# One pass over x removed, the hidden rows of the graph part made in the first attention stage, the preparation reordered

## The reference, cut to what matters

```python
xn = layernorm(x, eps=1e-5)
# graph part: rows that are gathered along the edges
h = relu(xn @ W1 + b1) @ W2 + b2            # 512 -> 256 -> 512
gnn = h + segment_sum(h[dst], src)
# attention part, one batch of 6250 tokens
k, q, v = split(layernorm(xn, eps=1e-3) @ kqv_w + kqv_b)
kp = exp(k @ w.T - |k|^2 / 2) / 16          # 256 features; qp in the same way from q
D = qp . sum_t kp ;  kptv = v.T @ kp
y = v + ((qp @ kptv.T) / D) @ proj_w + proj_b
mix = y + gelu(layernorm(y) @ mlp_w1) @ mlp_w2
x = x + gnn + mix
# then a Haar transform with two layers on its low half, on layernorm(x), added to x
```

## Time and profile before

| | us |
|---|---|
| median of 3 runs (2145.37 to 2147.61) | 2145.99 |
| the profiled execution | 2143.18 |
| its span, first to last instruction | 2141.4 |
| TensorE busy | 1913.4 (89%) |
| VectorE busy | 1184.4 (55%) |
| ScalarE busy | 493.2 (23%) |
| GpSimd busy | 1006.1 (47%) |
| mean granted TensorE clock | 0.954 |

### The profile page before, as it was taken

How to read it: one execution, slowest core, us unless ns; L and a number is a source line. 1 busy time by engine, 2 the same in 40 slices (tenths; PEclk the granted TensorE clock), 3 DMA queues, 4 the chain that set the end, 5 groups by cost and what they waited for, 6 DMA issues and landing times.

```text
span 2141.4 us, 24742 instructions
## 1 busy us (share of the span) xinstructions
PE 1913.4 (89%) x8639; PEld 1455.0 (68%) x8639; DVE 1184.4 (55%) x2337; ACT 493.2 (23%) x1083; POOL 1006.1 (47%) x1054
## 2 busy tenths in 40 slices
PE   3866699999979999999999997599999999999775
PEld 2755688888767777777777775466666666776432
DVE  3456398987234555555555554134444456665776
ACT  2445433333210111111111110111111122232222
POOL 3232200000056777777777777477777754410000
PEclk8878799999999999999999999699999999999997
DMA  7434522223223444444444445455555544432222
GB/s 207 165 120 160 160 85 68 80 81 93 69 79 110 134 137 137 137 136 137 137 136 136 137 128 171 134 156 160 162 165 161 179 150 156 155 125 99 91 96 82
DMA packets 90895, 278.93 MB, mean 130 GB/s; under 512 B 19183, under 2 KB 20719, under 8 KB 90774
## 3 DMA queue, kind: packets, MB, share of 16 engines
q1 hardware_dynamic: 46358, 153.81, 21.5%
q0 software_dynamic: 44416, 123.56, 21.4%
HBM read 232.47 MB, written 44.83 MB: 129 GB/s over the span
## 4 chain that ended last, share of the span: by engine, by line
PE 74%; DVE 10%; DMA 9%; issue 4%; ACT 1%; POOL 1%; DVEq 0%; SPq 0%; ACTq 0%
PE bank L777 8%; PE bank L784 8%; PE bank L683 8%; PE turn_bank L683 7%; PE bank L558 5%; PE bank L560 5%; PE bank L559 5%; PE bank L717 4%; PE bank L647 3%; DMA sb_step<-x_t 3%; DVE sb_weights L1084 3%; DMA out<-sb_step 2%; PE bank L696 2%; PE bank L698 2%; PE bank L697 2%
## 5 line engine op out<-in xcount | busy, mean ns | idle before, releaser
L496 POOL DMA_INDIRECT sb_weights<-hidden_rows,sb_weights x880 | 910.5, 1035 | 428.5 <-issue 245.2
L558 PE MATMUL bank<-sb_w_parts,sb_x_high 128*125 128x256 f32 (+1 forms) x700 | 242.2, 346 | 5.1 <-DVE sb_x_low L1151 5.1
L683 PE MATMUL bank<-sb_weights 128*125 128x257 f32 x880 | 231.7, 385 | 16.5 <-DVE sb_acc L1361 12.5
L1361 DVE TENSOR_TENSOR sb_acc<-sb_acc,bank 125x257 f32 x220 | 92.6, 421 | 264.9 <-PE bank L683 256.2
L560 PE MATMUL bank<-sb_w_parts,sb_x_low 128*125 128x256 f32 (+1 forms) x700 | 231.3, 330 | 0.0
L559 PE MATMUL bank<-sb_w_parts,sb_x_high 128*125 128x256 f32 (+1 forms) x700 | 231.3, 330 | 0.0
L683 PE MATMUL turn_bank<-sb_weights 128*125 128x257 f32 x880 | 229.8, 382 | 1.6 <-DMA sb_weights<-hidden_rows,sb_weights 1.4
L683 PEld LDWEIGHTS bank<-sb_weights 128*125 128x125 f32 x880 | 154.7, 187 | 69.3 <-issue 51.3
L777 PE MATMUL bank<-sb_weights 128*128 128x250 f32 x800 | 180.0, 378 | 15.7 <-issue 15.0
L683 PEld LDWEIGHTS turn_bank<-sb_weights 128*125 128x125 f32 x880 | 160.2, 187 | 33.1 <-issue 5.9
L784 PE MATMUL bank<-sb_weights,sb_step 128*125 128x512 f32 x400 | 177.8, 593 | 0.8 <-ACT sb_weights L1029 0.7
(11 more groups left out here) (229 smaller groups left out, 3056.1 us busy)
## 6 DMA issues: line engine op xcount, KB each, us to landing
sb_step<-x_t SPq DMA_DIRECT2D x75, 500.0 KB, 7.2
sb_step<-x SPq DMA_DIRECT2D x75, 500.0 KB
sb_weights<-hidden_rows,sb_weights POOLq DMA_INDIRECT x880, 3.7
y_rows<-sb_step SPq DMA_DIRECT2D x25, 500.0 KB
sb_step<-y_rows SPq DMA_DIRECT2D x25, 500.0 KB
z_rows<-sb_step SPq DMA_DIRECT2D x25, 500.0 KB
sb_step<-z_rows SPq DMA_DIRECT2D x25, 500.0 KB
out<-sb_step SPq DMA_DIRECT2D x25, 500.0 KB
```

The costliest lines, as they stand in the source:

```text
L496: pool.indirect_dma_start(out=slot(n, h), out_offset=None, in_=table, in_offset=bass.IndirectOffsetOnAxis(ap=row_of[:, n, h:h + 1], axis=0 ...
L558: pe.matmul(bk, high, rhs(0, c), start=c == 0, stop=False)
L683: mm = pe.matmul((BE, BH)[n % 2][0:P, 0:RW], hit[n // BP % 2][:, n % BP * 2 + h, :], slot(n, h), start=h == 0, stop=h == 1)
L1361: dve.tensor_tensor(dst, dst, (BE, BH)[n % 2][0:P, 0:RW], ALU.add).then_inc(g_add, 1)
```

## The change: what it does

- Pass 0 is gone. Steps of passes 1 and 2 alone load x.
- The W1 weights (r) lie between the k weights and the kqw weights in `w1_parts`, so that r and kqw come from one product of 512 columns (256 + 256) into a whole bank. It also waits until VectorE has read the r rows of the step before.
- VectorE reads each r half (`rt`) behind the kqw row of the same m; ScalarE applies ReLU and makes the row statistics of the next step; GpSimd makes `row_scales` within pass 1; SP stores the step's rows.
- The preparation of k, q and v stands ahead of pass 1; centring q and v is inside its step 0.
- 15 sort stages ahead of pass 1 (26 before), then parts of at most 5 stages.
- The ring lies in one piece in the place of all of `w1_parts`, so also the first gathers wait for the last product of pass 1.

```diff
-PRESORT = 26
+PRESORT = 15
-SORT_PARTS = sort_schedule(4)
+SORT_PARTS = sort_schedule(5)
...
         @block.sync
-            passes = [t for phase in range(3) for t in each_step(phase)]
+            passes = each_step(1) + each_step(2)
...
-            for t in each_step(0):
-                sp.wait_ge(st_sq, t.u + 2)
-                load_rows(passes[t.n + 2])
-                sp.wait_ge(r_mm, t.u + 2)
-                load_xt(passes[t.n + 2])
-                if t.u > 1:
-                    store_r(Step(0, t.u - 2))
...
                     load_rows(passes[t.n + 2])
+                store_r(t)
...
         @block.gpsimd
-            pool.wait_ge(r_in, 3 * 16)
             loads(w_in, ...)
+            loads(w2_in, ...)
+            loads(v_in, ...)
...
-            for t in each_step(0):
+            for t in each_step(1):
+                if t.u == SORTED + 1:
+                    pool.wait_ge(sort_ok, sort_ops(len(SORT)) + 1)
+                    pool.dma_start(iota_g, d["c_iota_g"]).then_inc(iota_in, 16)
                 row_scales(t)
...
-                    if n == 4:
+                    if n == 0:
                         pool.wait_ge(w_mm, STEPS * 2 + 1)
...
         @block.tensor
-            def r_products(t):
...
+            raw_products("k", k_raw, kt_raw, wt, BC, BD, (BE, BF))
+            pe.wait_ge(w2_in, 3 * 16)
+            pe.wait_ge(ev("gnn1_split"), 1)
+            raw_products("q", q_raw, qt_raw, wt, BG, BH, (BA, BB))
+            means("k", k_raw, folded_k, vb_k, wt, (BE, BF, BD))
+            pe.wait_ge(v_in, 3 * 16)
+            bias_row(BC, v_raw).then_inc(ev("v_raw"), 1)
+            means("q", q_raw, folded_q, vb_q, wt, (BG, BH[:, 0:M], BH[:, M:2 * M]))
+            pe.wait_ge(ev("v_gained"), 1)
+            mean(BC, v_raw, D).then_inc(ev("v_mean"), 1)
+            pe.wait_ge(ev("k_split"), 1)
...
                 pe.wait_ge(w_ok, t.g * 2 + 1)
-                product((BB, BF)[m][0:P, 0:M], t, m, w1_parts, WKW, M).then_inc(w_mm, 1)
+                pe.wait_ge(r_up, t.u * 2 + 1)
+                product((BB, BF)[m][0:P, :], t, m, w1_parts, WR, HID + M).then_inc(w_mm, 1)
...
         @block.scalar
+            high_parts(Step(1, 0), w_mm, 0)
+            stats(Step(1, 0))
+            stats(Step(1, 1))
             for t in each_step(1):
...
                 mm.then_inc(kpn_ok, 1)
+                act.wait_ge(r_up, t.u * 2 + 3)
+                act.activation(acc[0:P, t.u * 2:t.u * 2 + 2, 0:HID], rt[0:P], ACT.Relu).then_inc(r_ok, 1)
+                if 0 < t.u < STEPS - 1:
+                    stats(next_step(t))
...
         @block.vector
+            sort_stages(0, 3)
...
+            sort_stages(3, 8)
+            gains("k", k_raw, folded_k, vb_k, bk_bc, kqb[:, 0:KC], BC, BD, (BE, BF))
+            sort_stages(8, 13)
+            gains("q", q_raw, folded_q, vb_q, bq_bc, kqb[:, KC:2 * KC], BG, BH, (BA, BB))
...
+            low_parts(Step(1, 0))
...
+            centre_with_bias("k", k_raw, folded_k, bk_bc, bkw_bc, gram_k, half_k, w1_unused, (BE, BF, BD))
+            split_parts(k_raw, w1_parts, WK, D)
+            split_parts(folded_k, w1_parts, WKW, M)
+            dve.drain().then_inc(ev("k_split"), 1)
+            sort_stages(13, PRESORT)
...
             for t in each_step(1):
                 own1.start(t)
+                if t.u == 0:
+                    q_and_v()
+                    seq(dve.memset(kps[0:P], 0.0))
                 if t.u + 1 < STEPS:
                     low_parts(next_step(t))
+                dve.wait_ge(scaled, t.u + 2)
                 for m in (0, 1):
-                    kqw_rows(t, m, (BB, BF)[m][0:P, 0:M], bkw_bc, m + 1)
+                    kqw_rows(t, m, (BB, BF)[m][0:P, HID:HID + M], bkw_bc, m + 1)
+                    dve.wait_ge(r_ok, t.u + 1)
+                    dve.scalar_tensor_tensor(out=rt[0:P, m], in0=(BB, BF)[m][0:P, 0:HID], scalar=s1[0:P, t.u * 2 + m:t.u * 2 + m + 1],
+                                             in1=b1_bc[0:P, :], op0=ALU.mult, op1=ALU.add).then_inc(r_up, 1)
```

More of the change, by code:

```diff
@@ L24 @@
 ROUND = 12582912.0
-WK, WKW = 0, D
+WK, WR, WKW = 0, D, D + HID
 WQ, WV, WQW = 0, D, 2 * D
@@ L290, in build_program @@
         sort_ok, sort_tr = sem("sort_exchanges"), sem("keys_transposed")
-        split, r_mm, k_mm, w_mm, w_ok, sq, ex, nx, v_mm, kpn_ok = (sem(n) for n in (
-            "x_split", "r_products", "kq_products", "kqw_products", "kqw_rows", "kq_squared", "exps",
+        split, k_mm, w_mm, w_ok, sq, ex, nx, v_mm, kpn_ok = (sem(n) for n in (
+            "x_split", "kq_products", "kqw_products", "kqw_rows", "kq_squared", "exps",
             "square_sums", "v_products", "kp_scaled"))
@@ L496, in gathers @@
                         pool.indirect_dma_start(
-                            out=slot(n, h), out_offset=None, in_=table,
+                            out=ring[:, n % RING * 2 + h], out_offset=None, in_=table,
                             in_offset=bass.IndirectOffsetOnAxis(ap=row_of[:, n, h:h + 1], axis=0)
@@ L527, in _ @@
             pe.wait_ge(gnn_in, 16)
-            mean(BC, gnn1_raw, HID).then_inc(ev("gnn1_mean"), 1)
+            mean(BA, gnn1_raw, HID).then_inc(ev("gnn1_mean"), 1)
             def raw_products(name, raw, raw_t, wt, cols, row, folds):
@@ L561, in product @@
                 return mm
-            def r_products(t):
[L565 to L569, removed]
-            pe.wait_ge(ev("gnn1_split"), 1)
[L571 to L594, removed]
+            pe.wait_ge(w_in, 5 * 16)
+            pe.wait_ge(ev("bias_in"), 1)
+            raw_products("k", k_raw, kt_raw, wt, BC, BD, (BE, BF))
+            pe.wait_ge(w2_in, 3 * 16)
+            pe.wait_ge(ev("gnn1_split"), 1)
+            raw_products("q", q_raw, qt_raw, wt, BG, BH, (BA, BB))
@@ new lines, in _, with open_sums @@
+            means("k", k_raw, folded_k, vb_k, wt, (BE, BF, BD))
[5 more added lines that the diff above has]
+            pe.wait_ge(ev("k_split"), 1)
+            def open_sums():
+                pe.wait_ge(ev("qv_centred"), 1)
+                for bk in (BC, BD):
+                    pe.matmul(bk[:, :], zero_row[0:1, 0:128], zero_row[0:1, :].unsqueeze(1).to_broadcast([1, 2, M]),
+                              start=True, stop=False)
@@ L1179, in centre_with_bias @@
                 seq(mm)
+            dve.wait_ge(r_in, 3 * 16)
+            for k in range(KC):
+                dve.tensor_copy(vb4[:, k, :], n1b[:, k:k + 1].to_broadcast([128, 128]))
+            dve.drain().then_inc(ev("bias_in"), 1)
+            sort_stages(0, 3)
             dve.wait_ge(ev("gnn1_mean"), 1)
-            centre(gnn1_raw, BC, HID)
-            split_parts(gnn1_raw, wr_parts, 0, HID)
+            centre(gnn1_raw, BA, HID)
+            split_parts(gnn1_raw, w1_parts, WR, HID)
             seq(dve.memset(acc[0:P, :, HID:RW], 1.0))
@@ L1185, in _ @@
             dve.drain().then_inc(ev("gnn1_split"), 1)
-            low_parts(Step(0, 0))
-            w1_unused = LATE[:, 0:KC * D].rearrange("p (c n) -> p c n", c=KC)
-            w2_unused = ATT[:, 0:KC * D].rearrange("p (c n) -> p c n", c=KC)
-            def r_rows(t):
-                dve.wait_ge(r_mm, t.u + 2)
-                dve.wait_ge(scaled, t.u + 2)
-                dve.wait_ge(r_ok, t.u + 1)
-                for m in (0, 1):
-                    dve.scalar_tensor_tensor(out=rt[0:P, m], in0=(BA, BB)[t.u % 2][0:P, m * HID:(m + 1) * HID],
-                                             scalar=s1[0:P, t.u * 2 + m:t.u * 2 + m + 1],
-                                             in1=b1_bc[0:P, :], op0=ALU.mult, op1=ALU.add).then_inc(r_up, 1)
@@ L1277, in wait @@
                     pass
-            seq(dve.memset(kps[0:P], 0.0))
             def rank_part(u):
```

101 lines of the change are left out of this document (28 added, 73 removed).

## The result

The changed kernel takes 2060.76 us (median of 4 runs, 2059.57 to 2065.66); the kernel before took 2145.68 in the runs beside it. The ratio is 0.961, 95% interval [0.959, 0.964]. The forecast was 2062.5.

A forecast was written before the change was run, and what follows sets the result against it. The r pass was taken as bound by load latency, the first attention stage by nearly matched TensorE and VectorE. 89.7 us gained less 6.2 at the turn gave 83.5, so 2059.7 profiled and 2062.5 forecast; range 2046 to 2086.

The forecast's parts named there:

- k weights in: Preparation: k weights loaded at 30 us, bounds 27 and 38, with q and v weights queued behind them.
- first mark: VectorE's read of the second kqw row in the first attention stage's first step: 107.2 us instead of 267.99.
- stage by the step rule: First attention stage, 24 steps each costed by its longer engine: 376.1 us, plus 15.5 kept, gives 391.6.
- last mark: VectorE's read of the second kqw row in the stage's last step: 502.8 us, before 592.5, 89.7 gained.
- loss at the turn: Into the next stage: first gathers now wait for the last rows' store; 6.2 us lost (4 to 11).
- span, change: Whole profiled execution: 89.7 us gained at the last mark less 6.2 at the turn, 83.5.
- The 15.5 us that I carried over unsplit: Stage before the change: 324.5 measured against 309.0 by the step rule; the 15.5 left was kept in the forecast.
- POOL's row scales: Five small POOL instructions a step, moved into the stage, slow VectorE: 4 us, bounds 0 and 26.
- The rival at 2085: Stage: VectorE bounds all the sort's steps through POOL's instructions at their upper bound, 22 us more; chance 0.15.
- ScalarE's load and SP's store: Stage: ScalarE's row statistics and ReLU, SP's row store, costed at nothing; without ScalarE's cover, 3.7 us a step, 93.
- The rival "slower": Stage: engines alternate at the r rows, sort steps 21.8 us instead of 16, 104 more, 2167; chance 0.04.
- The preparation at half clock (2103): Preparation: TensorE keeps the half clock, its 41.5 us of products nearly double, weights land at 38; chance 0.08.

The follow-up runs named there:

- the first of the two runs: Changed kernel without the r half of the product (256 columns instead of 512) and VectorE's two reads of it: 2018.70 us, ratio 0.944.
- the second: Kernel before the change with its kqw products made 512 columns wide, the extra columns not read: 2199.74 us, ratio 1.028.
- the worst kernel: Changed kernel with six more small GpSimd instructions in each step of the stage: 2066.14 us, ratio 0.964; its first mark came at 115.20.

## Why the prediction was right

Term by term (us; forecast, measured):

| step of the prediction | forecast | measured |
|---|---|---|
| k weights in | 30 | 34.8 |
| k raw products, and their end | 18.6, 48.6 | 16.1, 50.9 |
| q raw products, and their end | 15.6, 64.2 | 13.9, 64.8 |
| means of k end | 71.1 | 71.7 |
| bias row of v end | 74.6 | 75.2 |
| low part of x end | 79 | 79.5 |
| k centred and split | 92.2 | 92.7 |
| first mark | 107.2 | 108.05 |
| stage by the step rule | 391.6 | 391.7 |
| POOL beside VectorE | 4 | 0 |
| last mark | 502.8 | 499.8 |
| store landed behind its issue | 3.7 | 4.1 |
| fourth pair's rows landed behind the mark | 19 | 19.1 |
| fourth group's products | 1 | 2.1 |
| fourth group's end behind the mark | 20 | 21.2 |
| loss at the turn | 6.2 | 7.4 |
| behind the turn | 0 | 1.6 longer |
| span, change | 83.5 | 83.8 |

The sum is closer than its terms, which is luck: the 4 us taken for POOL and not needed stand against 0.9 in the preparation, 1.2 at the turn and 1.6 behind it, and 0.3 is left.

- **The preparation** holds to 0.9 us, by errors that cancel. The row at 15.57 in the earlier trace rows is of two loads; the one that lands last was issued at 16.46 and in at 33.8, not 33. The k weights came 4.8 later than forecast, though POOL's 4.6 us of waiting did go away (this load was issued at 11.61, not 16.46): it took 23.2 us instead of 17.3, of which 2.6 is owed to q's and v's loads. The other 3.3 stay open. The share of busy DMA engines over the first 35 us doesn't explain them: it was 0.92 at 251 GB/s in the changed kernel (row below) and 0.69 at 191 GB/s in the kernel before, but with q's and v's loads held back it was 0.73 at 195 GB/s, nearly that of before, and the load still took 20.6. In return k's products took 16.1 where I had added 3 for the clock of the earlier trace rows, and q's took 13.9 where I had 15.6. That, too, is partly luck of the execution that was profiled: in the others k's took up to 20.3 and q's up to 17.3.
```profile
0.00:35.00 35.00, 3.92 (x9) 2.67 (x10) 16.46 (x37) 5.37 (x11) 14.40 (x28) 0.76 0.92 251
```

- **The stage** is the rule's sum to 0.1 us, which is partly luck. By the distances of the hk products, steps 1 to 3, given as 16.7, 16.7 and 16.3, came as 14.7, 16.3 and 18.0; 7 to 13, given as 15.4, as one 16.3 and six 15.5; 6, 14 and 16, given as 18.7, 16.6 and 17.9, as 19.5, 16.6 and 18.2. The 15.5 us that I carried over unsplit were needed again (391.7 - 376.1): two of the ranking steps behind the sort are 20.5 each, some 12 above the rule together, as they were before (17.7 and 17.8). That 42.7 us of the stage are r's (the earlier trace rows gives 65 if TensorE had bounded all of it) and that 53.8 were paid for the same columns in the kernel before shows what the step rule rests on: a column costs its time only as far as TensorE is the longer engine of the step. The rule was 4.9 off in the first of the two runs and 1.1 in the second.
- **POOL's row scales**, 4 us taken between 0 and 26: the only term that was wrong in what it says and not by a margin. The 0.9 us of the earlier trace rows were not POOL's at all. They are four operations of the sort's first stage, at 637 to 654 ns, beside four of the next at 419 to 430, and the changed kernel shows the same eight with no POOL instruction beside them: first row their ns min/median/max, second row the next that POOL runs, behind 16.14 us of idle time.

```profile
L1069 DVE SCALAR_TENSOR_TENSOR sb_weights<-sb_weights x8: 419/508/614, 23.9 to 27.1; 128x256 f32<-128x256 f32 x8
32.31 0.19 POOL L459 TENSOR_SCALAR sb_const<-sb_const 125x2 f32<-125x2 f32 x1 [16.14 <-ACT sb_step L868]
```

With nearly three times POOL's busy time the hk interval didn't move either. The rival at 2085 is refuted by that run, and not only by the time.
- **ScalarE's load and SP's store** were costed at nothing. ScalarE waits 92.3 us for TensorE and 52.8 for row scales and is busy 101 of 200 us; VectorE waited for its rounding 9.3 us in four pieces. The cover held.
- **The turn** is the new wait named, and its chain held: the fourth pair's rows landed 19.1 behind the mark. What I hadn't in the sum is the clock there, and nearly all of the 1.2 us are its: the fourth group's products took 2.07 against 1.03. The last hk products took 5.38 against 3.46, and the first 16 kptv products 6.28 against 5.47. The latter may be some of the 1.6 us lost behind the turn; but over the profiles that change nothing from there on this stretch was 1527.5 to 1530.6 us, so the 1.6 are within the scatter.
- The rival "slower", engines that alternate at the r rows, would have shown steps near 21.8 all through; the nine steps of 15.5 are against it. The preparation at half clock (2103) did show in part: 7 us late in the worst kernel, not 40.

Not tested: that the r pass was bound by the latency of its loads is read from the earlier trace rows, since the low part of x takes the place of the transposed x and a load can't be left out without changing what follows; that 89.7 us forecast for its removal came out as 92.8 agrees with it.

## What to carry to other kernels

A pass that is bound by the latency of its loads is cheap to merge into one that is bound by an engine: price the merged work per step by the longer engine of that step, not by the sum, and expect a part of it to fall into the other engine's steps (here 42.7 of 65 us were paid). Then look at the seam: what was fetched during the old stage and now must wait for its last rows is the loss (here 7.4 us), and moving the consumer behind work that doesn't need it takes it back, though what is moved is still paid. Idle time left in a preparation is the place for work with no due date: 8 sort stages moved there, with smaller parts, made the stage 10.9 us shorter. Before a long duration is put down to a neighbour, look whether the same instruction is as dear without it: the slow sort operations of the earlier trace rows were.

## What the runs showed of the hardware that was not expected

- A POOL instruction of 125x2 beside VectorE's two-input operations is itself stretched, from about 0.7 us to 0.8 to 0.9, while the VectorE operations stay at 0.69 us.
- TensorE, busy without a gap, ran at a granted clock of 1.00 in some executions and of 0.80 to 0.83 in others, 7 us of difference in the first mark; two executions of one and the same kernel differed by 1.6 us there.
- A store of 251 KB took 4.1 us from issue to landing, and the gather that waits for it began 0.8 us later.
- A load of 256 KB, one row spread over 128, took 8.7 and 10.5 us in one place and 20.6 in another of the same execution, 17.3 in the kernel before.
